# x's first half behind weight chunk 3 on SyncE's queue, and its low parts shared by VectorE and GpSimd

## What is computed

```python
A, Bm = lora_As[adapter_mapping], lora_Bs[adapter_mapping]          # 8 slots out of 32, rank 16
c = einsum('bti,oi->bto', x, W) + b + einsum('btr,bro->bto', einsum('bti,bir->btr', x, A), Bm) * 2
xf = c.reshape(1024, 512)
base = xf @ W_base.T + b_base
rw, sel = top_k(xf @ W_router.T, 2); rw = softmax(rw)               # 8 experts, 2 taken
w = einsum('tk,tke->te', rw, one_hot(sel, 8))
h = einsum('td,erd->ter', xf, A_ffn)                                # rank 16 per expert
out = x + (base + einsum('ter,te,eor->to', h, w, B) * 2)
```

## Time and profile before

| | |
|---|---|
| median of 3 runs | 69.98 us (69.63 to 70.16) |
| profiled execution | 69.86 us, of which the span of the trace is 68.0 us |
| TensorE busy | 63.3 us, 93% of the span |
| VectorE busy | 38.2 us, 56% |
| ScalarE busy | 23.8 us, 35% |
| GpSimd busy | 15.4 us, 23% |
| DMA | 8.45 MB, mean 124 GB/s; nearly all of the reading lies in the first 19 us |

### The profile page before, as it was taken

The page is one execution under the profiler, slowest core; times in us unless marked ns, Lnnn a source line. Parts: engine busy times, 40 slices in busy tenths (PEclk is TensorE's granted clock), DMA queues, the critical chain, the costliest instruction groups (busy, mean ns, idle before and its releaser), DMA issues.

```text
span 68.0 us, 1117 instructions
## 1 busy us (share of the span) xinstructions
PE 63.3 (93%) x393; PEld 57.2 (84%) x393; DVE 38.2 (56%) x106; ACT 23.8 (35%) x54; POOL 15.4 (23%) x28
## 2 busy tenths in 40 slices
PE   4999999999989959999999999999999999999940
PEld 4989899999969949988888879997887888898930
DVE  0066499990999890130699862103689891244620
ACT  0750777069995293770920202222210202000000
POOL 6800000000199933249970000200000000000000
PEclk9999999999999999999999999999999999999999
DMA  0899999967910005156420000000030714003462
GB/s 0 251 367 343 372 312 344 326 188 202 352 53 0 0 12 134 35 124 145 104 53 5 0 0 0 0 0 0 0 154 0 262 51 160 5 0 154 154 231 77
DMA packets 4634, 8.45 MB, mean 124 GB/s; under 512 B 652, under 2 KB 2316, under 8 KB 4629
## 3 DMA queue, kind: packets, MB, share of 16 engines
q1 hardware_dynamic: 4192, 7.17, 32.5%
q10 hardware_dynamic: 436, 1.22, 5.3%
HBM read 5.27 MB, written 2.10 MB: 108 GB/s over the span
## 4 chain that ended last, share of the span: by engine, by line
PE 60%; DMA 18%; POOL 7%; ACT 5%; DVE 3%; issue 2%; SPq 1%
PE ps L643 33%; DMA xt<-x_t 10%; PE ps L594 9%; DMA wt<-w_chunks 8%; POOL x_lo L251 6%; PE ps L596 3%; ACT x_hi L277 3%; PE ps L652 3%; PE ps L658 3%; PE ps L659 3%; PE ps L660 3%; PE ps L624 1%; PE ps L606 1%; SPq L196 1%; DVE bsum_hl L373 1%
## 5 line engine op out<-in xcount | busy, mean ns | idle before, releaser
L251 POOL TENSOR_TENSOR x_lo<-xt,x_hi 128x512 fp32r<-128x512 f32 x8 | 10.6, 1347 | 16.0 <-DVE bsum_hl L373 15.1
L643 PE MATMUL ps<-x_hi,m_lo 128*128 128x512 f32 (+1 forms) x36 | 9.7, 373 | 0.0
L643 PE MATMUL ps<-x_hi,m_hi 128*128 128x512 f32 (+1 forms) x36 | 9.2, 378 | 0.0
L594 PE MATMUL ps<-rt,x_hi 128*128 128x304 f32 x32 | 8.3, 346 | 0.8 <-POOL x_lo L251 0.8
L643 PE MATMUL ps<-x_lo,m_hi 128*128 128x512 f32 (+1 forms) x36 | 8.9, 368 | 0.0
L479 DVE TENSOR_TENSOR xt<-ps,xt 128x512 f32<-128x512 f32 (+1 forms) x9 | 5.6, 629 | 4.7 <-PE ps L660 4.7
L596 PE MATMUL ps<-rt,x_lo 128*128 128x152 f32 x32 | 7.5, 234 | 0.0
L643 PEld LDWEIGHTS ps<-x_lo,m_hi 128*128 128x128 f32 x36 | 6.4, 188 | 1.2
L517 PE MATMUL ps<-wt_hi 128*128 128x324 f32 x32 | 7.1, 328 | 0.0
L643 PEld LDWEIGHTS ps<-x_hi,m_hi 128*128 128x128 f32 x36 | 6.2, 188 | 1.0
L643 PEld LDWEIGHTS ps<-x_hi,m_lo 128*128 128x128 f32 x36 | 6.2, 188 | 0.9
(11 more groups left out here) (73 smaller groups left out, 98.9 us busy)
## 6 DMA issues: line engine op xcount, KB each, us to landing
out_t<-xt SPq DMA_DIRECT2D x7, 256.0 KB, 2.0
wt<-w_chunks SPq DMA_DIRECT2D x3, 582.0 KB, 6.5
xt<-x_t ACTq DMA_DIRECT2D x2, 512.0 KB, 6.2
xt<-x_t SPq DMA_DIRECT2D x2, 512.0 KB, 6.0
g_st<-g_hl SPq DMA_DIRECT2D x12, 81.0 KB, 2.1
ab<-adapters SPq DMA_DIRECT2D x8, 64.0 KB, 4.5
btt<-b_t SPq DMA_DIRECT2D x1, 256.0 KB, 3.9
out_t<-xt SPq DMA_DIRECT2D x2, 128.0 KB, 1.7
```

The lines of the kernel that those rows point to most:

```text
L251: nc.gpsimd.tensor_tensor(x_lo[:, h, k, :], xt[:, h, k, :], x_hi[:, h, k, :].bitcast(F32), ALU.subtract).then_inc(x_lo_done, 1)
L594: mm(t_banks(p)[:, t, 0:2 * TA], x_hi[:, h, i, tok], op, start=(i == 0), stop=False, skip_group_check=True)
L643: mm(piece_ps(n), a[:, i, o * P:(o + 1) * P], v[:, h, i, tok], start=(m == 0), stop=False)
```

## The change

x's first half is issued by SyncE behind chunk 3 and ahead of chunk 4, and no longer by ScalarE after chunk 2's high parts. ScalarE makes `x_hi` of row blocks 0 and 1 between chunk 3 and chunk 4 and those of blocks 2 and 3 after chunk 4. VectorE makes `x_lo` of blocks 0 and 1, after the last bias sum and ahead of `bs_lo`. GpSimd makes those of blocks 2 and 3, both ahead of the copies of adapter tables. The second half of x is split as before. Nothing is computed differently.

```diff
         @block.sync
             for n in (0, 2):
                 sp.dma_start(wt[:, 0, W0_PIECES[n]], w[:, 0, W0_PIECES[n]]).then_inc(w0_in[n], 16)
-            sp.dma_start(wt[:, 1, :], w[:, 1, :]).then_inc(w_in[1], 16)
-            for k in range(2, KB):
+            for k in range(1, KB - 1):
                 sp.dma_start(wt[:, k, :], w[:, k, :]).then_inc(w_in[k], 16)
+            for k in range(0, KB, 2):
+                sp.dma_start(xt[:, 0, k:k + 2, :], x[:, 0, k:k + 2, :]).then_inc(x_in[0], 16)
+            sp.dma_start(wt[:, KB - 1, :], w[:, KB - 1, :]).then_inc(w_in[KB - 1], 16)
         @block.gpsimd
-            x_split(0, range(KB - 1))
+            x_split(0, range(2, KB))
             pool.wait_ge(ab_hi_done, 2)
             pool.wait_ge(ab_lo_done, 2)
             put_adapter(0)
             put_adapter(1)
-            x_split(0, (KB - 1,))
         @block.scalar
-            for k in range(1, KB):
+            def w_high(k):
                 act.wait_ge(w_in[k], 16)
                 hi(wt_hi[:, k, D:CH], wt[:, k, D:CH]).then_inc(wc_hi_done, 1)
                 hi(wt_hi[:, k, 0:D], wt[:, k, 0:D]).then_inc(w_hi_done, 1)
-                if k == 1:
-                    for n in range(0, KB, 2):
-                        act.dma_start(xt[:, 0, n:n + 2, :], x[:, 0, n:n + 2, :]).then_inc(x_in[0], 16)
+            w_high(1)
+            w_high(2)
             act.wait_ge(x_in[0], 32)
-            for k in range(KB):
-                hi(x_hi[:, 0, k, :], xt[:, 0, k, :]).then_inc(x_hi_done, 1)
+            x_high(0, 0)
+            x_high(0, 1)
+            w_high(3)
+            x_high(0, 2)
+            x_high(0, 3)
         @block.vector
             bias_sum(KB - 1)
+            for k in range(2):
+                dve.wait_ge(x_hi_done, k + 1)
+                lo(x_lo[:, 0, k, :], xt[:, 0, k, :], x_hi[:, 0, k, :]).then_inc(x_lo_dve, 1)
             dve.wait_ge(ab_hi_done, 1)
         @block.tensor
                 if p == 0:
                     pe.wait_ge(x_hi_done, KB)
-                    pe.wait_ge(x_lo_done, KB)
+                    pe.wait_ge(x_lo_dve, 2)
+                    pe.wait_ge(x_lo_pool, 2)
```

More of the change, by code:

```diff
@@ L152, in build @@
         x_hi_done = sem("x_hi_done")
-        x_lo_done = sem("x_lo_done")
+        x_lo_dve = sem("x_lo_dve")
+        x_lo_pool = sem("x_lo_pool")
         m_done = sem("m_done")
@@ L251, in x_split @@
                     nc.gpsimd.tensor_tensor(x_lo[:, h, k, :], xt[:, h, k, :], x_hi[:, h, k, :].bitcast(F32),
-                                            ALU.subtract).then_inc(x_lo_done, 1)
+                                            ALU.subtract).then_inc(x_lo_pool, 1)
             def put_adapter(b):
@@ L290, in _, with x_high @@
                 hi(wt_hi[:, k, 0:D], wt[:, k, 0:D]).then_inc(w_hi_done, 1)
-                if k == 1:
-                    for n in range(0, KB, 2):
-                        act.dma_start(xt[:, 0, n:n + 2, :], x[:, 0, n:n + 2, :]).then_inc(x_in[0], 16)
+            def x_high(h, k):
+                hi(x_hi[:, h, k, :], xt[:, h, k, :]).then_inc(x_hi_done, 1)
+            w_high(1)
+            w_high(2)
             act.wait_ge(x_in[0], 32)
-            for k in range(KB):
-                hi(x_hi[:, 0, k, :], xt[:, 0, k, :]).then_inc(x_hi_done, 1)
+            x_high(0, 0)
[3 more added lines that the diff above has]
+            x_high(0, 3)
             act.wait_ge(ab_in, 16 * NB)
@@ L315, in _ @@
                 hi(bsum_hl[0:1, 0, s * WH:(s + 1) * WH], ps[0:1, C_BANK + s, 0:WH]).then_inc(c_hi_done, 1)
-            def x1_hi(k):
-                hi(x_hi[:, 1, k, :], xt[:, 1, k, :]).then_inc(x_hi_done, 1)
             def take_part(p):
@@ L338, in _ @@
             act.wait_ge(x_in[1], 32)
-            x1_hi(0)
-            x1_hi(1)
+            x_high(1, 0)
+            x_high(1, 1)
             take_part(0)
-            x1_hi(2)
-            x1_hi(3)
+            x_high(1, 2)
+            x_high(1, 3)
             take_part(1)
@@ L586, in router @@
                     pe.wait_ge(x_hi_done, 2 * KB)
-                    pe.wait_ge(x_lo_done, 2 * KB)
+                    pe.wait_ge(x_lo_pool, 2 + KB)
                 for t in range(2):
```

## The result

| | before | changed |
|---|---|---|
| median, 19 runs each | 69.89 us | 70.28 us |
| ratio, 95% interval | | 1.0077 [1.0049, 1.0106] |
| span of the profiled execution | 68.0 us | 68.3 us |
| GpSimd busy | 15.4 us | 12.5 us |
| VectorE busy | 38.2 us | 39.4 us |

The changed kernel is slower by 0.8%, about 0.54 us. That is less than the 1% that was named as what one can tell, but with 19 runs on each side the interval excludes both no change and a gain.

A forecast was written before the change was run, and what follows sets the result against it. TensorE, busy 93% of the span, bounds the kernel, with holes of 0.48 us ahead of G and 0.94 ahead of the router. Router +0.6 on 69.86 gives 70.45, against the median 70.6; 70.5 given, range 69.8 to 71.3.

The forecast's parts named there:

- The landing of chunk 4: SyncE's queue: 1.05 MB of x goes ahead, so ScalarE starts on chunk 4 at 13.3 us instead of 10.20.
- ScalarE and the adapter tables stay out of it: ScalarE is free when chunk 4 lands; the tables come by 16.5, `bs_hi` is needed at 18.4: cover 1.9 us.
- VectorE's list: VectorE's work behind chunk 4, including two added `x_lo` of 1.26 us, starts `bs_lo` at 18.4, 1.5 us later.
- D: Start of VectorE's `bs_lo`, the clock for G and the router; forecast t + 5.13 = 18.4 us, against 16.91.
- t: Landing of chunk 4, seen as ScalarE's start on it; forecast 13.3 us, bounds 12.95 to 13.7, against 10.20.
- TensorE: M ends at 19.2, G waits for VectorE until 21.05; the hole ahead of G grows from 0.48 to 1.8 us.
- GpSimd: Two `x_lo` end at about D + 4.1, adapter copies at D + 5.3, closing the hole ahead of the router.
- The router, and what follows it: Router starts at 25.25 to 25.3 instead of 24.68, +0.6 us; stacked tables still fit ahead of `slots(0)` by 0.5.
- B (faster): Chunk 4 lands early, t below 12.7; at 11.7 the 0.94 us hole is fully gained, 69.0 us; chance 0.07.
- C (level): VectorE's shift and GpSimd's relief cancel, with t near 12.7: 69.8 to 70.1 us; chance 0.11.
- D, the late tables: Stacked tables take 3.3 us to land instead of 2.1, `slots(0)` waits 0.7 more: 71.3 us; chance 0.09.
- E, the clock: TensorE's clock falls after the hole ahead of G; G and bias take 8.0 instead of 4.1 us: 74; chance 0.06.

The follow-up runs named there:

- the bias sum moved ahead: Changed kernel with chunk 3's bias sum moved ahead of chunk 4's low parts on VectorE; ratio to the kernel before 0.9996.
- the load order alone: Changed kernel with the split of low parts undone, so GpSimd makes all four `x_lo`; ratio to the kernel before 1.0093.
- half of x ahead: Changed kernel with only the first of x's two transfers ahead of chunk 4, and ScalarE on chunk 4 before x; ratio to the kernel before 0.9938.
- `x_lo` ahead of chunk 4's low parts: Changed kernel with VectorE's two `x_lo` moved ahead of its low parts of chunk 4; measured twice, ratios to the kernel before 0.9973 and 0.9956.

## Why the prediction was right, step by step

The forecast was 70.5 us with 69.8 to 71.3, slower by 0.6 in the router's start. The measurement is 70.28, the shift 0.51 in the router and 0.54 in the ratio.

1. **The landing of chunk 4.** 13.3 forecast, 13.31 in the profile. The eight profiles with these transfers range from 13.17 to 13.99, with 13.53 in the middle, so that the hundredths agree is luck. And the two terms in it were both off, against each other. The changed kernel's windows show (same columns as the earlier trace rows):

```profile
3.00:9.00 6.00, 5.93 (x39) 5.40 (x38) 3.04 (x8) 2.79 (x6) 0.38 (x4) 1.00 0.99 319
0.00:12.00 12.00, 10.94 (x76) 10.40 (x77) 6.16 (x13) 4.97 (x8) 2.60 (x12) 1.00 0.85 282
...
12.00:13.00 1.00, 1.00 (x9) 1.00 (x8) 0.48 (x1) 0.95 (x2) 0.00 (x0) 1.00 1.11 343
```

   By 12.0 us 12.0 x 282 = 3.38 MB were moved, so the 3.43 MB were complete at 12.15 and not at 11.8, as the rate from 3 to 9 us was 319 and not 361 GB/s. From 7 to 12 us, the stretch that the forecast needed, it was 339. The lag behind the last byte was 1.2 and not 1.45. The sum is right partly by chance. The fixed cost of about 2.0 us that the Trainium skill gives ("DMA: Bandwidth & Descriptors", "Anatomy of one DMA — SWDGE (gpsimd) path") is stated there for transfers that GpSimd issues. As the lag of one from SyncE's queue it would have been further off than the rows' 1.45.
2. **ScalarE and the adapter tables stay out of it.** Right: `x_hi` of blocks 0 and 1 were done at 12.95, and `bs_hi` started at 15.64 without a wait on the tables.
3. **VectorE's list.** D = 18.4 forecast, 18.38 measured; D - t = 5.13 forecast, 5.07 measured. The `x_lo` took 0.60 from start to start, for 0.63. The experiments confirm the term by its count (one, two, three) and by its place, and the bias sum moved ahead shows that it is the length of the list that counts. One wait was not seen: `bsum_hl` behind ScalarE, 0.27 us. It was covered in the changed kernel and would have been needed for the load order alone.
4. **TensorE.** G at 21.05 forecast, 20.97 measured. M ended at 19.44 and not at 19.2, because chunk 2's high parts began at 7.31 and not at 6.93. The hole was 1.5 instead of 1.8, which changes nothing as G waited for VectorE.
5. **GpSimd.** Its copies end at D + 5.25, forecast D + 5.3. The hole that the change aims at is closed.
6. **The router, and what follows it.** 25.25 forecast, 25.19 measured. `slots(0)` did not wait for the stacked tables; how much of the slack was left was not measured. From the router on, the changed kernel's profile gets back 0.2 us: the last `xt` of VectorE starts at 65.74, 0.3 behind the 65.42 of the kernel before. The router's matmul pairs followed each other every 0.250 us instead of 0.253, and the first pair, which did not come out of a wait, took 0.07 less. I did not test why; between the two kernels' 19 runs the difference is 0.54, close to the router's shift of 0.51, which is that of one profile on each side.

**The rivals.** B (faster) and C (level) needed t at 12.7 or below, and half of x ahead shows that they had the right mechanism: with t = 12.2 the kernel is faster than before. D, the late tables, did not occur. E, the clock, did not occur in the changed kernel's 25 executions, but it came with a hole 0.7 us longer. Its price was put too high: 1.56 us and not 3.9, as TensorE ran at full rate for the first 1.6 us of G and was back at it before the bias matmuls. The chances for slower than 70.7 do not add up as written: 0.3, 0.09 and 0.06 are 0.45 and not 0.41. The forecast does not depend on it.

## What to carry to other kernels

A transfer that is brought forward in a queue pushes back all that stood there, so look first at what the pushed transfer releases and how much work stands behind it on the engine that is released last. Moving work from a late engine to an idle one is only worth something while the idle time lies where the work can be done: the same two instructions were worth -1.1 us with the weights first and nothing with x first. Of two edits made together, run each alone before judging either: here one was a gain of 1.5% and the other a loss of 0.9%.

## What the runs showed of the hardware

- The clock of TensorE fell 1.6 us after the end of a hole of 2.2 us, with the matmuls of 324 columns 0.27 instead of 0.15 us apart for 3.4 us. That is one profile; the mean granted clock gives two such executions of six. With holes of 1.5 and 1.6 us in the changed kernel's two profiles, all of its 25 executions kept 0.999 or more. For the same kernel this gives two groups of times about 2 us apart (72.5 and 72.6 against 69.9 to 71.0), which the mean granted clock (0.976 against 0.995 and above) tells apart.
- The granted clock does not show every stretch at the lower rate. In the first profile of `x_lo` ahead of chunk 4's low parts the matmuls of M were 0.27 us apart from 6.2 to 9.7, and with half of x ahead from 5.2 to 6.8, while the granted clock reads 1.00. In the kernel before and in the changed one they were 0.15 apart from 4.9 and 5.4 on. The distance between matmuls is the surer sign. What decides how long it lasts was not tested.
- VectorE's `as_hl`, a subtraction with two inputs in SBUF, took 1.19 to 1.24 us in the eleven profiles in which GpSimd was in the middle of an `x_lo` when it came. It took 0.68 in the first profile of `x_lo` ahead of chunk 4's low parts, where GpSimd's two were over, and 0.69 with three `x_lo` on VectorE, where GpSimd's only one ran from 20.80 to 22.07:

```profile
22.65 0.69 DVE L379 TENSOR_TENSOR as_hl<-ab,as_hl 128x512 fp32r<-128x512 f32 x1
```

  Where GpSimd had a third `x_lo` to follow, as before, that one was stretched to 1.75. The Trainium skill has the rule ("SBUF — State Buffer", "SBUF: two separate sides"): GpSimd and a VectorE instruction with two SBUF inputs exclude each other for a whole instruction. The rows agree.
- The landing of one and the same early chunk differed from one execution to the next by up to 1.45 us (ScalarE's start on chunk 2 lay between 6.81 and 8.26 in the profiles of kernels whose transfers up to it are the same). In six of the thirteen profiles M ended 12.12 to 12.18 us behind that start, in the others 12.25 to 14.20 behind it. How much of this reaches the end of the kernel was not measured.
